# Layer 0's loads and the scaling of its heads reordered, the tail's heads normalised by two engines, the recurrent block's last products laid among the last experts, and output additions in two column halves

## What is computed

```python
x = L0_attn_x
xn = _layernorm(x, axis=-1)
x = x + _L0_attn_ref(xn, ...) + _L0_ffn_ref(xn, ...)
xn = _layernorm(x, axis=-1)
x = x + _L1_attn_ref(xn, ...) + _L1_ffn_ref(xn, ...)
...
# in _L0_attn_ref, for each group of dv // nh = 8 columns
o = (o32 * jax.lax.rsqrt(jnp.mean(o32 * o32, axis=-1, keepdims=True) + EPS)).astype(o.dtype)
o = o.reshape(b, nh, s, dv) * (1.0 - L_INIT)
...
# _L1_attn_ref
r = jax.nn.silu(x @ Wr)
f = jax.nn.sigmoid(x @ Wf)
c = jax.nn.silu(x @ Wc)
_, h = jax.lax.associative_scan(combine, (f, c), axis=1)
y = r * rmsnorm(h, ln_scale) @ Wo
...
# _L1_ffn_ref
scores = jax.nn.softmax(logits.astype(jnp.float32), axis=-1)
topk_w, topk_idx = jax.lax.top_k(scores, K)
...
hmid = jax.nn.silu(gate) * up
yb = jnp.einsum('ecf,efh->ech', hmid, w_down).reshape(E * CAP, h)
...
out = jnp.zeros((T, h), yb.dtype).at[slot_token].add(slot_out)
```

## Time and profile before

| what | us |
|---|---|
| runs | 3387.91, 3388.32, 3391.61 (median 3388.32) |
| profiled execution, own time | 3390.38 |
| its span, first to last instruction | 3387.2 |
| PE busy | 3142.5 (93% of the span) |
| DVE, POOL, ACT busy | 1831.7, 1612.4, 1259.3 |
| first part | 0 to 55.7 |
| layer 0 | 55.7 to 2502.5 |
| tail: its heads and router logits | 2502.5 to 2592.4 |
| tail: routing beside projections | to 2686 |
| tail: experts | to the end |

### The profile page before, as it was taken

The page is one execution under the profiler, slowest core; times in us unless marked ns, Lnnn a source line. Parts: engine busy times, 40 slices in busy tenths (PEclk is TensorE's granted clock), DMA queues, the critical chain, the costliest instruction groups (busy, mean ns, idle before and its releaser), DMA issues. The chain is left out here.

```text
span 3387.2 us, 45436 instructions
## 1 busy us (share of the span) xinstructions
PE 3142.5 (93%) x16170; PEld 2427.2 (72%) x16170; DVE 1831.7 (54%) x3864; ACT 1259.3 (37%) x2829; POOL 1612.4 (48%) x1410
## 2 busy tenths in 40 slices
PE   4999999899999999999999899999958999999996
PEld 3777777677777777877777777777735667776764
DVE  4556656655655566565556656555635553434431
ACT  3444444434434342434334243433424223233322
POOL 2366657634645653364455335455541263444442
PEclk8999999999999999999999999999978999999998
DMA  6433322353222234221112522211144677787885
GB/s 207 160 114 109 106 81 100 131 171 122 75 97 90 85 128 148 87 81 63 63 69 103 159 82 73 77 63 69 38 154 169 188 199 192 205 203 223 203 216 110
DMA packets 219389, 424.74 MB, mean 125 GB/s; under 512 B 22432, under 2 KB 103072, under 8 KB 217120
## 3 DMA queue, kind: packets, MB, share of 16 engines
q1 hardware_dynamic: 200608, 377.79, 33.5%
q0 software_dynamic: 18560, 44.05, 7.0%
HBM read 311.09 MB, written 110.69 MB: 125 GB/s over the span
## 5 line engine op out<-in xcount | busy, mean ns | idle before, releaser
L775 POOL TENSOR_SCALAR probs<-probs,comb 128x512 f32<-128x512 f32 (+3 forms) x384 | 221.6, 586 | 1011.7 <-DVE comb L724 1011.1
L896 ACT ACTIVATE probs<-score_ps,neg_max 128x640 f32<-128x640 f32 (+7 forms) x512 | 374.4, 738 | 475.1 <-DVE neg_max L730 475.1
L730 DVE TENSOR_REDUCE neg_max<-score_ps 128x2 f32<-128x256 f32 (+7 forms) x256 | 347.3, 1357 | 101.2 <-PE score_ps L1023 100.1
L780 POOL TENSOR_TENSOR probs<-probs 128x512 f32<-128x512 f32 (+3 forms) x384 | 384.1, 1014 | 10.7
L784 POOL TENSOR_TENSOR out_root<-out_root,neg_half 128x16 f32<-128x16 f32 x128 | 372.6, 2911 | 5.6 <-DVE out_root L707 5.6
L819 ACT ACTIVATE attT<-turn_ps 128x512 fp32r<-128x512 f32 (+3 forms) x384 | 188.9, 492 | 463.3 <-PE turn_ps L932 461.0
L631 DVE TENSOR_TENSOR layer_sum<-product_ps,layer_sum 128x512 f32<-128x512 f32 x384 | 263.2, 685 | 31.9 <-PE product_ps L40 26.0
L1020 PE MATMUL score_ps<-keys_all,queries_all 64*128 64x512 f32 (+3 forms) x2304 | 277.9, 364 | 0.0
L618 DVE TENSOR_TENSOR attT<-turn_ps,attT 128x512 fp32r<-128x512 f32 (+3 forms) x384 | 212.9, 555 | 102.3 <-ACT attT L819 99.3
L677 DVE SCALAR_TENSOR_TENSOR hidden<-gate_tanh,product_ps 128x512 f32<-128x512 f32 x128 | 88.0, 688 | 312.2 <-ACT gate_tanh L861 312.2
L1020 PEld LDWEIGHTS score_ps<-keys_all,queries_all 64*128 64x128 f32 x2304 | 187.4, 186 | 75.0 <-issue 44.3
(11 more groups left out here) (280 smaller groups left out, 7294.0 us busy)
## 6 DMA issues: line engine op xcount, KB each, us to landing
w_qk<-weights_split SPq DMA_DIRECT2D x48, 512.0 KB, 4.6
w_gate<-weights_split SPq DMA_DIRECT2D x48, 512.0 KB, 3.3
w_up<-weights_split SPq DMA_DIRECT2D x48, 512.0 KB, 3.5
w_down<-weights_split SPq DMA_DIRECT2D x48, 512.0 KB, 6.7
e_gate_up<-in_w_gate_dram SPq DMA_DIRECT2D x64, 384.0 KB, 3.7
e_gate_up<-in_w_up_dram SPq DMA_DIRECT2D x64, 384.0 KB, 5.0
e_down<-in_w_down_dram SPq DMA_DIRECT2D x64, 384.0 KB, 4.9
values_by_head<-hidden_split SPq DMA_DIRECT2D x32, 512.0 KB, 3.3
```

What stands on the lines that cost most here:

```text
L730: dve.tensor_reduce(nmax[:, i % 2, :], score_tile(i % NT), AX.X, ALU.max, negate=True)\
L775: pool.tensor_scalar(PR[:, r, 1, c], PR[:, r, 1, c], comb[:, i % 4:i % 4 + 1], 1.0, ALU.mult, ALU.mult)\
L780: pool.tensor_tensor(PR[:, r, 0, c], PR[:, r, 0, c], PR[:, r, 1, c], ALU.add).then_inc(s_comb, 1)
L896: act.activation(PR[:, i % 2, q, 0:(j + 1) * P], score_tile(j)[:, q, :], ACT.Exp, bias=nmax[:, i % 2, q:q + 1], accum_out=sums[:, i % 16, ...
```

## The change

Five edits, in the order of the program.

1. Layer 0's opening loads: lambda, identity and mask are issued first, then two tiles of x, three pieces of weights, and the six other tiles; the eight loads of `Y` move into slots 3 to 10 of the opening.
2. On DVE in layer 0, the scaling of the heads (L689) with its wait stands ahead of the group's L667 and L670 and of gate and up (L677, L682), no longer behind them.
3. The tail's heads: even tiles are normalised on DVE and odd ones on ACT, both two tiles ahead; the first two stand ahead of the router weights' copy. A batch's first logit stands behind its fifth head, its second behind the second head of the next batch.
4. The gaps of 10 and 20 are gone; the one of 8 stays. The plan is the same up to the stage with the last projections. In it experts 52 to 56 have projection products too, experts 57 to 60 none, expert 61 has the last power and three output products, expert 62 three with the first `yadd`, expert 63 two.
5. Each addition into the result becomes two, of the left and the right 256 columns, with its own chain each (`s_chain[0]`, `s_chain[1]`): two indirect DMAs of 1 KB rows for an expert in place of one of 2 KB rows, two DMAs for each `yadd`. Their row numbers, `halves`, are made by two more small DVE instructions. An ACT evacuation that reuses a tile waits for both chains.

```diff
+                sp.dma_start(lam_sb[:, :, :], lam).then_inc(s_c, 16)
+                sp.dma_start(ident[:, :], ident_d).then_inc(s_c, 16)
+                sp.dma_start(hf[:, 0, 0:P], mask_d[:, 0:P]).then_inc(s_c, 16)
                 for t in range(2):
-                    load_x(0, t)
-                sp.dma_start(ident[:, :], ident_d).then_inc(s_c, 16)
-                for t in range(2, NT):
                     load_x(0, t)
                 for n in range(3):
                     load_piece(n)
-                sp.dma_start(hf[:, 0, 0:P], mask_d[:, 0:P]).then_inc(s_c, 16)
-                sp.dma_start(lam_sb[:, :, :], lam).then_inc(s_c, 16)
-                for t in range(NT):
-                    load_y(0, t)
...
+                    if hb == 0 and 3 <= s < 3 + NT:
+                        load_y(0, s - 3)
...
+                        if pair_at(i):
+                            k, t = pair_at(i)
+                            n = b * GROUPS + k * NT + t
+                            o_g = O[:, t, :].rearrange("p (g n) -> p g n", n=8)
+                            dve.wait_ge(s_oroot, n + 1)
+                            dve.scalar_tensor_tensor(o_g, o_g, 1.0 - L_INIT,
+                                                     grp[:, t % 4, :].unsqueeze(2).to_broadcast([P, 16, 8]),
+                                                     ALU.mult, ALU.mult).then_inc(s_on, 1)
...
-                        if pair_at(i):
-                            k, t = pair_at(i)
-                            n = b * GROUPS + k * NT + t
-                            o_g = O[:, t, :].rearrange("p (g n) -> p g n", n=8)
-                            dve.wait_ge(s_oroot, n + 1)
-                            dve.scalar_tensor_tensor(o_g, o_g, 1.0 - L_INIT,
-                                                     grp[:, t % 4, :].unsqueeze(2).to_broadcast([P, 16, 8]),
-                                                     ALU.mult, ALU.mult).then_inc(s_on, 1)
...
-            yield ("router",), 0
             for b in range(batches):
                 for t in range(NT):
-                    yield ("head", b, t), 0.95
+                    yield ("head", b, t), 0.75
+                    if b and t == 1:
+                        yield ("logit", b - 1, 1), 2.7
                     if b and t == 3:
                         yield ("cols", b - 1), 0.9
-                for h in range(2):
-                    yield ("logit", b, h), 2.7
+                    if t == 4:
+                        yield ("logit", b, 0), 2.7
+                if b == 0:
+                    yield ("router",), 0
+            yield ("logit", batches - 1, 1), 2.7
+
...
-                else:
-                    yield ("gap",), 10.0
...
-                        yield ("gap",), 20.0
...
+                    if v[0] == "head" and v[2] % 2 == 0:
+                        dve += 0.55
...
+                        for h in range(2):
+                            dve.tensor_scalar(halves[:, h, :], tmp[:, :], pad[:, h:h + 1], 2.0, ALU.add, ALU.mult).then_inc(s_slot, 1)
...
+                def normalise(n):
+                    b, t = divmod(n, NT)
+                    dve.wait_ge(s_shift, b + 1)
+                    dve.wait_ge(s_xa[b % 2][t], 16 * (b // 2 + 1))
+                    dve.tensor_scalar(x_tile(b, t), x_tile(b, t), rstd[:, b, t:t + 1], shift[:, b, t:t + 1], ALU.mult, ALU.add)\
+                       .then_inc(s_xn[0], 1)
+
+                normalise(0)
...
+                        if v[0] == "head" and v[2] % 2 == 0 and v[1] * NT + v[2] + 2 < NTT:
+                            normalise(v[1] * NT + v[2] + 2)
...
                 def scatter(n):
                     pool.wait_ge(s_ys, n + 1)
-                    if link["expert", n]:
-                        pool.wait_ge(s_chain, 16 * link["expert", n])
-                    pool.indirect_dma_start(out, bass.IndirectOffsetOnAxis(slots[:, n:n + 1], 0), ys[:, n % 3, :], None,
-                                            compute_op=ALU.add).then_inc(s_chain, 16)
+                    for h in range(2):
+                        if link["expert", n]:
+                            pool.wait_ge(s_chain[h], 16 * link["expert", n])
+                        pool.indirect_dma_start(out.rearrange("t (h n) -> (t h) n", h=2),
+                                                bass.IndirectOffsetOnAxis(halves[:, h, n:n + 1], 0),
+                                                ys[:, n % 3, h * (D // 2):(h + 1) * (D // 2)], None,
+                                                compute_op=ALU.add).then_inc(s_chain[h], 16)
...
                             o, q = v[1:]
                             pool.wait_ge(s_ppe, pp["outp", o, 4 * q + 3] + 1)
-                            if link[v]:
-                                pool.wait_ge(s_chain, 16 * link[v])
-                            pool.dma_start(tile_rows(out, TURNS[o], 4 * q, 4).rearrange("(t p) n -> p t n", p=P), Y[:, q],
-                                           accum_op=ALU.add).then_inc(s_chain, 16)
+                            for h in range(2):
+                                part = slice(h * (D // 2), (h + 1) * (D // 2))
+                                if link[v]:
+                                    pool.wait_ge(s_chain[h], 16 * link[v])
+                                pool.dma_start(tile_rows(out, TURNS[o], 4 * q, 4)[:, part].rearrange("(t p) n -> p t n", p=P),
+                                               Y[:, q, :, part], accum_op=ALU.add).then_inc(s_chain[h], 16)
...
-                        normalise(0, 0)
-                        normalise(0, 1)
...
-                        b2, t2 = (b, t + 2) if t + 2 < NT else (b + 1, t - NT + 2)
-                        if b2 == b:
-                            normalise(b2, t2)
+                        if t % 2 and b * NT + t + 2 < NTT:
+                            normalise(b * NT + t + 2)
...
-                        if h == 1 and b + 1 < batches:
-                            normalise(b + 1, 0)
-                            normalise(b + 1, 1)
...
                 act.wait_ge(s_c, 64)
+                normalise(1)
...
                         if b == 0 and h == 0:
+                            pe.wait_ge(s_w, 16)
+                        if b == batches - 1 and h == 0:
                             pe.wait_ge(s_wl, 1)
```

More of the change, by code:

```diff
@@ L534, in _ @@
                     load_piece(n)
-                sp.dma_start(hf[:, 0, 0:P], mask_d[:, 0:P]).then_inc(s_c, 16)
-                sp.dma_start(lam_sb[:, :, :], lam).then_inc(s_c, 16)
-                for t in range(NT):
-                    load_y(0, t)
+                for t in range(2, NT):
+                    load_x(0, t)
                 for b, i, hb, s in phases():
@@ L1123, in tail @@
         slots = sb("slots", [P, E], I32)
+        halves = sb("slot_halves", [P, 2, E], I32)
         ident = sb("t_ident", [P, P])
@@ L1186, in tail @@
         s_tst = [[sem(f"xn_stored{p}_{t}") for t in range(NT)] for p in range(2)]
-        s_mv_in, s_var, s_root, s_shift, s_xn = (sem(n) for n in ("mv_in", "var", "root", "shift", "xn"))
+        s_mv_in, s_var, s_root, s_shift = (sem(n) for n in ("mv_in", "var", "root", "shift"))
+        s_xn = [sem("xn_even"), sem("xn_odd")]
         s_again = [sem(f"xn_again{t}") for t in range(4)]
@@ L1201, in tail @@
         s_xg = [sem(f"e_xg{q}") for q in range(XG)]
-        s_chain = sem("added")
+        s_chain = [sem("added_left"), sem("added_right")]
         s_xp, s_eT, s_wt, s_gu, s_sg, s_hm = (sem("e_" + n) for n in ("xp", "xT", "wt", "gu", "sg", "hm"))
```

34 lines of the change are left out of this document (20 added, 14 removed).

## The result

The changed kernel takes 3422.6 us (median of 4 runs, 3411.5 to 3423.6) where before takes 3388.1 (3384.1 to 3391.6): ratio 1.0095, 95% interval 1.0071 to 1.0118. I had forecast 3381, in a range of 3346 to 3395. The profiled execution is the quickest of the four, 3411.5 us with a span of 3409.7. Its mean granted clock is 0.967, while the three others have 0.963 or 0.964 and take 3421.8 to 3423.6.

What follows compares the result with a forecast made beforehand. The prediction took PE, busy 93% of the span, as the bound, so edits pay only where it stands still or runs at the lower clock. Terms -7 + 20 - 14 - 9 + 3 = -7 took 3388.3 to 3381 us, range 3346 to 3395.

Steps and rivals of the forecast that it cites:

- Edit 1, -7: Layer 0's opening loads: with lambda issued first, PE's first product comes 7 us earlier; range -4 to -8.
- My lower end, -4: Layer 0's opening loads: the smallest gain allowed, -4 us, if moving the eight tiles delays weight pieces on SP's queue.
- Edit 2, +20: Layer 0's scaling ahead of the gate: L792 still blocks it, making gate and PE later; 20 us slower in sum.
- My sign for the whole layer: Layer 0 as a whole, 75 to 2502, was to grow by 15 to 25 us, else the prediction is wrong.
- The first rival: Layer 0's scaling: DVE starts before L792, so 16 us are gained in place of 20 lost; 3345 us, chance 0.16.
- Edit 3, -14: Tail's heads: two normalising engines and interleaved logits remove 11 us idle, 1.5 from an earlier first head, 1.5 from clock.
- Edit 4, -9: Last experts and output products: removing the gaps covers waits for gathered rows and raises the clock; -9 us, -5 to -14.
- The matmuls themselves only move: Last experts and closing output products: matmuls only change place; 4.4 us of the 13.4 us idle and clock cost stay.
- Edit 5, +3: Additions into the result: a second scatter issue per expert, mostly hidden on POOL, costs 3 us; range 0 to +12.
- The third rival: Tail's experts: POOL's second issues become PE's wait, costing 23 us in place of 3; 3401 us, chance 0.10.
- halves landing side by side gain hardly anything: Closing chain of additions: 4.2 us of a transfer do not depend on size, so splitting hardly shortens the end.

Runs made afterwards that it cites:

- s_nudge2: Kernel before with the heads' scaling moved ahead of the gate, plus six short POOL memsets holding L792 back: 3369.1 us, ratio 0.9947.
- s_pad: Kernel before without the gaps of 10 and 20, but with 30 added to the cost shared out over the experts: 3382.2 us, ratio 0.9983.
- s_pad15: Kernel before without the gaps of 10 and 20, with 15 added to the shared cost: 3404.2 us, ratio 1.0034.
- s_halves: Kernel before with only the additions into the result split into two column halves: 3392.7 us, ratio 1.0008.
- s_gaps: Kernel before with only the gaps of 10 and 20 taken out: 3414.5 us, ratio 1.0069.

## Why the prediction was wrong

Alone, the edits measure -1, +25, -19, +24 and +2.5 us, +32 in sum, against +34.5 for the whole; they add up. The forecast is 42 us too low, and 33 of them are in edit 4's term. By my terms:

- **Edit 1, -7: measured -1.** The first product came 7.5 us earlier, as worked out. The step that failed is that a lead at the start is a lead at the end: of 7.5 us 4.2 were left at the first scaling, and in the edit's own trial none by 880 us. My lower end, -4, was still too hopeful. (Lambda stood behind thirteen transfers, not seventeen.)
- **Edit 2, +20: measured +25.** Mechanism right, down to the start 0.07 us behind L792 and the gate's 0.6 us, and the size within my range. The wait for L618 grew by 22.7 us, where I had lowered 21.6 to 18 for slack; I had counted 36 slots, and 44 turns wait longer. My sign for the whole layer, a growth of 15 to 25 us, came out at 29.0, since the lead of edit 1 went as well; from the first scaling on it is 25.7. The first rival needed DVE to start first; where it does (s_nudge2) the kernel gains 22 us in place of the 16 that I gave it, but the wait falls only to 51.1 us, where I had put it near 45.
- **Edit 3, -14: measured -19.** Direction right, reason not. I put 11 us on waits and 1.5 on the clock; it was 3.6 us of idle time and 16 of busy time, at a clock of 0.92 for 0.73. The clock of 1.00 in runs of logits and 0.50 in runs of heads stood in the earlier trace rows, and I did not ask what mixing them would give.
- **Edit 4, -9: measured +24.** This is the step that failed. I wrote "The matmuls themselves only move", and the text ahead of the prediction has it that the plan stays the same up to the last projections. It does not: a turn moves from expert 1 to expert 2, and from expert 16 to 59 every slot differs. A gap is a cost in the sum that is shared out (`allowed`), so it fattens the share of every expert ahead of it. Without 30 of it each later expert has less beside it, and up to expert 48 PE stands still for 18.6 us more, at a clock of 0.94 for 0.98. The last experts won part of my 9 us: from expert 48 on PE is idle for 4.5 us less, and the end behind the last weighting takes 22.5 us in place of 23.8. s_pad and s_pad15, with their traces up to expert 48, show that the share is the cause.
- **Edit 5, +3: measured +2.5.** The number is right, and can't be told from none; the reason is right only in half. The third rival, POOL's second issue as the wait, did not happen. But I had written that halves landing side by side gain hardly anything, and in s_halves the end is 3.4 us shorter, against 4.9 us more among the experts: that they nearly cancel is luck. In the changed kernel the halves run two by two at the end, and the time from the last weighting to the end is 19.1 us in place of 23.8, of which edit 4 alone brings 1.3:

```profile
3395.41 1.64 POOL L1848 DMA_INDIRECT out_dram<-e_y,slot_halves  x1 [3.86 <-DMA out_dram<-rec_out]
3397.93 1.55 POOL L1848 DMA_INDIRECT out_dram<-e_y,slot_halves  x1 [0.89 <-DMA out_dram<-rec_out]
3400.01 1.53 POOL L1848 DMA_INDIRECT out_dram<-e_y,slot_halves  x1 [0.53 <-issue]
3402.00 1.54 POOL L1848 DMA_INDIRECT out_dram<-e_y,slot_halves  x1 [0.47 <-DMA out_dram<-e_y,slot_halves]
```

The Trainium skill's rule, page "SBUF — State Buffer", section "Who interferes with whom", that issue order decides who blocks for a whole instruction, is borne out for DVE here: its scaling takes 1.35 us when L792 starts 0.07 us earlier, and 0.29 us when L792 starts 0.15 us later. That L792 is kept out in its turn does not show: its record is 1.3 us long in both orders.

## What to carry to other kernels

A cost without an item in a planner is a decision about every slot ahead of it: before it is taken out, compare the whole plan, not the place where it stood. An instruction that waits for another engine's result can lose the race against what that engine has queued right behind (here all 49 times); where the trace shows that the two slow each other, put something short and harmless between, or swap them. And where narrow and wide matmuls alternate by stage at different clocks, try to interleave them before looking for waits to remove.

## What was not expected of the hardware

- Six memsets of 128x8, which hold L792 back by 0.2 us, change the kernel by 47 us (3415.6 to 3369.1). They decide who starts first in 49 of the 128 scalings.
- The five waits of PE of 3.5 us in s_gaps are followed by 3.5 us at a mean granted clock of 0.55 to 0.71. By the highest of these it is an estimated 1 us more (0.29 x 3.5) that no wait shows.
- Runs of one kernel differ with the mean granted clock: over 17 runs of the kernel before, from 3382.8 us at 0.968 to 3400.2 us at 0.961. The changed kernel's profiled run, 10 us under its others, is such a case, so one profile shows only part of a difference of this size.
- What remains open: why edit 1's lead of 6.6 us is gone by 880 us, where the 11.6 us of busy time go that s_nudge2 saves, and by which waits the thinner share costs its 24 us.
